# Outlook stage: TensorE's other work cut into pieces behind the replications, the next chunk's softmax chain moved, a fourth accumulating transfer, filler matmuls in idle slots

## The chip, the cores and the metric

The kernel runs on one core of one Trainium2 chip, in one launch. The metric is the device time of the whole launch in microseconds (us). The kernel before takes 4110.46 us (median of three runs, 4110.16 to 4110.85). The engines are named as the profile names them: PE is TensorE (matmuls; PEld its weight loads), DVE is VectorE, ACT is ScalarE, POOL is GpSimd, SP is SyncE.

## The reference, cut to what matters

The input is a batch of 16 images of 56 x 56 pixels and 192 channels. Two blocks follow each other, each on a group-normalised input and with a residual. The first, an "outlook attention", is the one that the change touches:

```python
def _L0_conv_ref(x_map, W_attn, b_attn, W_v, b_v, W_proj, b_proj):   # heads 6, K 3, 32 channels a head
    a = x_map @ W_attn + b_attn
    a = jax.nn.softmax(a.reshape(B, H * W, heads, k * k), axis=-1)      # 9 weights per pixel and head
    v = x_map @ W_v + b_v
    vp = jnp.pad(v, ((0, 0), (pad, pad), (pad, pad), (0, 0)))
    patches = jnp.stack([vp[:, i:i + H, j:j + W, :] for i in range(k) for j in range(k)], axis=3)
    y = jnp.einsum('bpKhd,bphK->bphd', patches, a)                      # sum over the 9 taps
    return y.reshape(B, H, W, C) @ W_proj + b_proj

x = x + _L0_conv_ref(_gn(x), ...)
x = x + _L1_conv_ref(_gn(x), ...)      # shifted 7 x 7 window attention, 12 heads
```

## The kernel before

The 16 images are taken in 8 pairs. A pair fills the partitions: 2 x 192 channels are three tiles of 128, called j = 0, 1, 2, where tile 1 holds 64 channels of each image (`LO` and `HI` are its halves). A loop over the 8 pairs has two stages: the outlook stage (about 173 us of the 502 us of a pair in the trace) and the window attention stage. The change touches the outlook stage alone.

The outlook stage goes through 7 chunks of 8 image rows (448 pixels), c = 0 to 6. In a chunk the nine taps k = 0 to 8 are 14 operations (`OPS`, `NOPS`). For operation n, PE replicates the softmax weights over the channels with one or two bf16 matmuls against a selection matrix (`reps`, line 409), into one of two pairs of PSUM banks, and DVE multiplies this by the shifted values (`product`, line 1237) into a slot of `prod`. `reps(c, n)` waits until product n-2 is done, since it takes the banks of that one. So PE can be two operations ahead of DVE, no more. Below, "slot n" of a chunk is the replication n and what PE does behind it until replication n+1.

The nine products are summed in two ways. POOL issues three DMAs that add one slot of `prod` to another (`merge`, line 1438: tap 1 onto 0, 3 onto 2, 5 onto 4; 672 KB each), and adds the rest itself (`add`, line 1453) into `psum_p` and at last `y0`. `FREED` says after which add a slot of `prod` may be written again; DVE waits for that, and for the transfers (`merged`), before a product.

Beside the replications PE does for the next chunk, c+1: `logits` (matmuls of the normalised input `xn` with W_attn), `values_wide` and `values_middle` (with W_v), `turn_logits` (transposes), and after the softmax `turn_weights` (transposes of the three bf16 parts of the weights, kept by ACT into `at`). And for the chunk before, c-1: `residual`, `project_halves`, `project_outer`, `project_middle` (the residual by an identity matmul, then W_proj). The order in which these stand between the replications is written by hand: by the `if n == ...` in `outlook` of PE, of DVE (softmax pieces) and of ACT. Each engine works strictly down its list, so an instruction that waits holds up all that stand behind it, the replications too. A matmul of 128 rows and 448 columns in fp32 goes as two records in the trace; two matmuls on the two halves of the array (as lines 334 and 335) run beside each other, below "a half pair".

In chunk 0 there is nothing to project, in chunk 6 nothing to prepare. Behind chunk 6 stand `finish_last` on DVE and two short additions on POOL (the last sums), then the last projection. `stay_warm` are matmuls whose result nobody reads.

Of the kernel before, what the change touches and what calls it, by code (L numbers as in the profile page):

```python
# [9 lines left out]
ALU = mybir.AluOpType  # L10
# [3 lines left out]
B, H, W, C = 16, 56, 56, 192  # L14
# [7 lines left out]
T = 3  # L22
LO, HI = slice(0, 64), slice(64, 128)
ORDER = (0, 2, 1)

OHEADS, KK = 6, 9
# [6 lines left out]
CHUNKS = H // ROWS  # L33
CT = ROWS * W
# [4 lines left out]
MERGES = 3  # L39
# [13 lines left out]
SUM_ORDER = (0, 2, 6, 8, 4, 7)  # L53
FREED = {0: 1, 2: 1, 6: 2, 3: 3, 4: 4, 7: 5}
# [26 lines left out]
def mixer(nc, x, wa, ba, wv, bv, wp, bp, wqkv, bqkv, wo, bo, table, sel_in, gmat_in, mask_in, out):  # L81
    ctx = ExitStack()
    with ctx:
# [202 lines left out]
        def _(pe):  # L286
# [43 lines left out]

            def logits(G, bank):
                pe.wait_ge(xn_ok, ONE + T * (G + 1))
                pe.wait_ge(a_kept, ONE + 2 * G)
                mm(P[LO, bank, 0:CT], wa_s[:, 0, :], xn[:, 0, :], start=True, stop=False)
                mm(P[HI, bank, 0:CT], wa_s[:, 2, :], xn[:, 2, :], start=True, stop=False)
                mm(P[LO, bank, 0:CT], wa_s[LO, 1, :], xn[LO, 1, :], start=False, stop=True)
                mm(P[HI, bank, 0:CT], wa_s[HI, 1, :], xn[HI, 1, :], start=False, stop=True).then_inc(l_mm, 1)
# [6 lines left out]
            def values_middle(bank):  # L344
                middle(bank + 1, wv_s, 0, 3, xn, CT).then_inc(v_mm, 1)

# [50 lines left out]
            with pe.Fori(0, NP) as i:  # L397
# [15 lines left out]
                def residual(c, tiles):  # L413
                    for j in tiles:
                        mm(P[:, V_BANK + j, 0:CT], ident[:], xa[:, j, c * ROWS:(c + 1) * ROWS, 0:W],  # L415
                           start=True, stop=False)

                def project_halves(c):
                    if c < CHUNKS - 1:
# [20 lines left out]

                def outlook(c):
                    G = G0 + c
                    more = c < CHUNKS - 1
                    for n in range(NOPS):
                        reps(c, n)
                        if more:
                            if n == 0:
                                logits(G + 1, SOFT_BANK)
                            elif n == 1:
                                pe.wait_ge(a_kept, ONE + 2 * G + 2)  # L450
                                pe.wait_ge(x1_kept, ONE + T * (G - 1 if c else G))
                                values_wide(V_BANK)
                            elif n == 2:
                                turn_logits(G + 1, SOFT_BANK)
                            elif n == 4:
                                values_middle(V_BANK)
                        if c > 0:
                            if n == 5:
                                pe.wait_ge(v_kept, ONE + T * (G + 2 if more else G + 1))
                                pe.wait_ge(x1_kept, ONE + T * (G - 1))  # L460
                                residual(c - 1, (0,))
                            elif n == 6:
                                residual(c - 1, (2, 1))
                            elif n == 7:
                                project_halves(c - 1)
                            elif n == 8:
                                project_outer(0)
                            elif n == 9:
                                project_outer(2)
                            elif n == 10:  # L470
                                project_middle(0)
                            elif n == 11:
                                project_middle(1)
                        if more:
# [1132 lines left out]
```

## Time and profile before

| | before |
|---|---|
| median of 3 runs | 4110.46 us |
| the profiled execution: its time / its span | 4108.7 / 4106.8 us |
| PE, DVE, ACT, POOL busy | 86%, 68%, 46%, 62% of the span |
| granted TensorE clock, mean | 0.918 of full speed |
| transfers `prod` onto `prod` | 168, 672 KB each, median 5.3 us from issue to landing |
| one pair, from the first product of pair 1 to that of pair 2 | 598.16 us on, period about 502 us |
| its outlook stage: first product to last sum | 598.16 to 770.04 us |

The page's shares are averages over two stages with different limits, so they say little of the outlook stage; the trace is read in stretches of one chunk of pair 1. The granted clock has two levels, 1.00 (2.4 GHz) and 0.50 (1.2 GHz); a number between them in a stretch is a mix.

### The profile page before, as it was taken

The numbers are of one execution on the slowest core, as the hardware profiler recorded it, in microseconds if no ns is written. First come the engines' busy times: TensorE is split into PE (matmuls) and PEld (weight loads), VectorE is DVE, ScalarE is ACT, GpSimd is POOL, SyncE is SP. The second block draws the span as 40 slices with busy tenths as digits, with TensorE's granted clock in tenths as the row PEclk, the third lists the DMA queues.
The fourth block names the chain that finished last, engine by engine and source line by source line (L and its number), as shares of the span: only waits on it lengthen the run. The fifth ranks groups of instructions, "written<-read, shape, count | busy, mean of one in ns | idle before, by whom it ended". The sixth has DMA issues, their size and how long they took to land.

```text
span 4106.8 us, 107056 instructions
## 1 busy us (share of the span) xinstructions
PE 3542.4 (86%) x39508; PEld 1954.8 (48%) x39508; DVE 2790.4 (68%) x4865; ACT 1897.6 (46%) x4034; POOL 2527.0 (62%) x1878
## 2 busy tenths in 40 slices
PE   4889978899788997889978899788997899978998
PEld 3336643366434663346633466335662356523565
DVE  2767757677576775857757577585776767667676
ACT  2325643355433554336633455334653255532555
POOL 0757737577375773757737577375764767556674
PEclk8989989899798997989979899798998999988998
DMA  3432214322242222422224222341223422134121
GB/s 73 88 71 67 77 47 88 66 63 75 52 88 60 70 70 62 90 55 75 72 54 88 52 75 70 63 90 46 76 68 68 81 59 77 53 78 85 50 76 56
DMA packets 199422, 284.55 MB, mean 69 GB/s; under 512 B 18136, under 2 KB 177368, under 8 KB 198872
## 3 DMA queue, kind: packets, MB, share of 16 engines
q0 software_dynamic: 24192, 115.62, 14.4%
q1 hardware_dynamic: 168992, 160.51, 13.2%
q8 instruction: 343, 5.62, 0.6%
q10 hardware_dynamic: 5688, 1.11, 0.2%
q14 instruction: 207, 1.70, 0.1%
HBM read 45.97 MB, written 38.54 MB: 21 GB/s over the span
## 4 chain that ended last, share of the span: by engine, by line
PE 58%; issue 14%; DVE 11%; ACT 9%; POOL 5%; DVEq 1%; ACTq 0%; DMA 0%; POOLq 0%
PE P L292 5%; PE P L294 5%; PE P L409 4%; PE P L582 4%; PE P L599 4%; PE P L553 4%; PE P L415 3%; DVE prod L1237 3%; PE P L295 3%; PE P L532 3%; PE P L301 3%; PE P L535 2%; PE P L300 2%; PE P L617 2%; POOL sp__70 L1522 2%
## 5 line engine op out<-in xcount | busy, mean ns | idle before, releaser
L1237 DVE TENSOR_TENSOR prod<-P,vpad 128x896 f32<-128x896 f32 (+1 forms) x784 | 807.2, 1048 | 343.8 <-PE P L409 342.2
L1515 POOL TENSOR_TENSOR sp__70<-sp__70,mx 128x588 f32<-128x588 f32 x512 | 599.9, 1172 | 622.2 <-DVE mx L1309 621.9
L1522 POOL TENSOR_TENSOR sp__70<-sp__70,rc 128x588 f32<-128x588 f32 x512 | 600.3, 1172 | 54.6 <-DVE rc L1319 54.6
L409 PE MATMUL P<-at,sel 108*128 108x448 bf16 x1512 | 453.9, 384 | 131.4 <-DVE prod L1237 71.2
L1438 POOL DMA_DIRECT2D prod<-prod x168 | 148.7, 885 | 660.3 <-DVE prod L1237 649.9
L1299 DVE TENSOR_TENSOR sp__70<-P,relb 128x196 f32<-128x196 f32 x512 | 184.7, 361 | 498.0 <-PE P L553 497.7
L974 ACT ACTIVATE pt<-P 98x294 f32<-98x294 f32 x1024 | 430.2, 421 | 200.6 <-PE P L582 197.8
L1453 POOL TENSOR_TENSOR psum_p<-psum_p,prod 128x1344 f32<-128x1344 f32 x152 | 461.8, 3038 | 11.9
L582 PE MATMUL P<-ident,sp__70 113*98 113x113 f32 x3072 | 399.2, 267 | 49.0 <-POOL sp__70 L1522 36.3
L1316 DVE TENSOR_REDUCE sm<-sp__70 128x12 f32<-128x588 f32 x512 | 387.3, 756 | 44.0 <-ACT sp__70 L964 43.9
L582 PEld LDWEIGHTS P<-ident,sp__70 113*98 113x98 f32 x3072 | 329.9, 131 | 145.4 <-POOL sp__70 L1522 71.8
L1309 DVE TENSOR_REDUCE mx<-sp__70 128x12 f32<-128x588 f32 x512 | 389.5, 761 | 9.4
L964 ACT ACTIVATE sp__70<-sp__70 128x588 f32<-128x588 f32 x512 | 360.6, 704 | 29.2 <-POOL sp__70 L1515 27.9
L409 PEld LDWEIGHTS P<-at,sel 108*128 108x128 bf16 x1512 | 115.5, 100 | 512.9 <-DVE prod L1237 270.9
L553 PE MATMUL P<-kbd,qs 32*64 32x98 f32 x12288 | 305.5, 264 | 24.7 <-ACT kbd L948 12.6
L1302 DVE TENSOR_TENSOR sp__70<-P,relb 128x392 f32<-128x392 f32 x512 | 284.5, 556 | 0.0
L958 ACT ACTIVATE vs<-P 98x192 f32<-98x192 f32 x512 | 126.7, 333 | 294.7 <-PE P L532 294.7
L553 PEld LDWEIGHTS P<-kbd,qs 32*64 32x64 f32 x12288 | 205.0, 133 | 111.2 <-issue 95.2
L1508 POOL TENSOR_SCALAR xr<-xa,bout 128x392 f32<-128x392 f32 x192 | 246.5, 1285 | 0.0
L599 PE MATMUL P<-pt,vbd 98*32 98x49 f32 x12288 | 221.2, 218 | 24.6 <-ACT pt L974 18.0
L415 PE MATMUL P<-xa,ident 128*128 128x448 f32 x336 | 164.0, 604 | 75.4 <-ACT vpad L840 74.8
L898 ACT ACTIVATE xa<-P,bias 128x448 f32<-128x448 f32 x168 | 106.7, 635 | 262.9 <-PE P L428 209.2
(185 smaller groups left out, 7507.8 us busy)
## 6 DMA issues: line engine op xcount, KB each, us to landing
prod<-prod POOLq DMA_DIRECT2D x168, 672.0 KB, 5.3
vbd<-vs SPq DMA_DIRECT2D x512, 147.0 KB
xin<-in_x SPq DMA_DIRECT2D x126, 336.0 KB, 4.0
out<-ot SPq DMA_DIRECT2D x184, 168.0 KB, 2.2
out<-ot SPq DMA_DIRECT2D x80, 84.0 KB
wn<-in_L_conv_qkv_weight SPq DMA_DIRECT2D x2, 432.0 KB, 6.4
wno<-in_L_conv_proj_weight SPq DMA_DIRECT2D x2, 144.0 KB, 6.5
self<-in_sel ACTq DMA_DIRECT2D x3, 91.1 KB
```

Of the source, the lines that this page charges most:

```text
L409: last = mm(P[:, 2 * (n % 2) + b, 0:CT], sel[:, k, :], at[:, col:col + CT], start=True, stop=True)
L553: last = mm(P[half * SLOT:(half + 1) * SLOT, r, part * 2 * N:(part + 1) * 2 * N], qs[rows, w % 2, j, tok:tok + SLOT], kbd[rows, w % 2, j, ...
L582: last = turn(P[0:2 * N, bank, c * QUERIES:(c + 1) * QUERIES], sp_[0:QUERIES, s % SOFTS, g * 2 * N:(g + 1) * 2 * N], ident[0:QUERIES, 0:QU ...
L599: last = mm(P[32 * r:32 * r + 32, Y_BANK, col:col + N], vbd[w % 2][:, 2 * p + half, m, 2 * HD * g:2 * HD * (g + 1)], pt[:, (q + m) % KEPT, ...
L964: go(sp_[:, s % SOFTS, :], sp_[:, s % SOFTS, :], ACT.Exp).then_inc(p_exp, 1)
L974: go(pt[:, (STEPS * w + s) % KEPT, 3 * b:3 * b + 3, :, :], src, ACT.Copy).then_inc(p_kept, 1)
L1237: tt(by_row(dst), by_row(P[:, b:b + len(op), 0:CT]), val, ALU.mult).then_inc(prod_ok, 1)
L1309: red(mx[:, b, :], sp_[:, b, :].rearrange("p (h k) -> p h k", h=NH), AX.X, ALU.max).then_inc(t_max, 1)
L1316: red(sm[:, b, :], sp_[:, b, :].rearrange("p (h k) -> p h k", h=NH), AX.X, ALU.add).then_inc(p_sum, 1)
L1453: tt(y0[:] if n == PADD - 1 else psum_p[:], slot(0) if n == 0 else psum_p[:], slot(k), ALU.add).then_inc(padd_ok, 1)
L1515: tt(per_head(sp_[:, b, :]), per_head(sp_[:, b, :]), spread(mx[:, b, :]), ALU.subtract).then_inc(t_sub, 1)
L1522: tt(per_head(sp_[:, b, :]), per_head(sp_[:, b, :]), spread(rc[:, b, :]), ALU.mult).then_inc(p_norm, 1)
```

## The change

In words:

- PE: `logits` is cut in two (slots 0 and 1 in place of slot 0 alone), the values in five pieces (slots 2, 4, 5, 5, 6 in place of 1 and 4), the order of value tiles becomes 0, 1, 2 (`V_ORDER`). The residual moves from slots 5 and 6 to 7 and 8, the projection from 7 to 11 to slots 9, 10 and 12, tiles in the order 2, 0, 1 (`P_ORDER`). `turn_weights` part 0 moves from slot 12 to 11.
- PE: two filler matmuls (`stay_warm(2, ...)`) in slots 8, 9, 10 and 12 of chunk 0, and in all slots but 7, 8, 9, 10 and 12 of chunk 6.
- DVE: softmax pieces from slots 3, 4, 6, 7, 9, 11 to 4, 5, 6, 7, 8, 9; the three statistics from slots 0, 1, 2 to 0, 5, 10.
- POOL: a fourth transfer a chunk (tap 7 onto 6) in place of one addition, in all chunks but the last; order of the additions changed; the last sums of the stage take tap 6 where they took tap 4.
- ACT: `back` part 1 ahead of the first `keep_x1`, `keep_weights` part 0 ahead of the last.

The core of the diff:

```diff
-MERGES = 3
+MERGES = 4
 PADD = KK - 1 - MERGES
-SUM_ORDER = (0, 2, 6, 8, 4, 7)
-FREED = {0: 1, 2: 1, 6: 2, 3: 3, 4: 4, 7: 5}
+FREED = {0: 1, 2: 1, 3: 2, 4: 3, 6: 4}
...
+                def prepare(c, n):
+                    G = G0 + c
+                    if n < 2:
+                        logits_part(G + 1, n, SOFT_BANK)
+                    elif n == 2:
+                        pe.wait_ge(a_kept, ONE + 2 * G + 2)
+                        pe.wait_ge(x1_kept, ONE + T * (G - 1 if c else G))
+                        values_halves(V_BANK)
+                    elif n == 3:
+                        turn_logits(G + 1, SOFT_BANK)
+                    elif n == 4:
+                        values_square(V_BANK)
+                    elif n == 5:
+                        values_outer(0, V_BANK)
+                        values_rest(V_BANK)
+                    elif n == 6:
+                        values_outer(2, V_BANK)
+                    elif n == 11:
+                        turn_weights(G + 1, 0, SOFT_BANK)
+                    elif n == 13:
...
+                        turn_weights(G + 1, 1, V_BANK)
+
+                def project(c, n):
+                    G = G0 + c
+                    if n == 7:
+                        if c < LAST:
+                            pe.wait_ge(v_kept, ONE + T * (G + 1) + 1)
+                        pe.wait_ge(x1_kept, ONE + T * (G - 1))
+                        residual(c - 1, 0)
+                    elif n == 8:
+                        if c < LAST:
+                            pe.wait_ge(v_kept, ONE + T * (G + 1) + 3)
+                        residual(c - 1, 2)
+                        residual(c - 1, 1)
+                    elif n == 9:
+                        project_halves(c - 1)
+                        project_middle(0)
+                    elif n == 10:
+                        project_outer(2)
+                        project_outer(0)
+                    elif n == 12:
+                        project_middle(1)
+
                 def outlook(c):
                     for n in range(NOPS):
                         reps(c, n)
+                        if c < LAST:
+                            prepare(c, n)
+                        elif n not in (7, 8, 9, 10, 12):
+                            stay_warm(2, SOFT_BANK)
                         if c > 0:
+                            project(c, n)
+                        elif n >= 8 and n not in (11, 13):
+                            pe.wait_ge(v_kept, ONE + T * (G0 + 2))
+                            stay_warm(2, V_BANK)
...
@@ ACT
                         back(G + 1, 0, SOFT_BANK)
+                        back(G + 1, 1, SOFT_BANK)
                     if c > 0:
                         keep_x1(c - 1, 0)
-                    if more:
-                        back(G + 1, 1, SOFT_BANK)
-                    if c > 0:
-                        keep_x1(c - 1, 1)
-                        keep_x1(c - 1, 2)
-                    if more:
-                        keep_weights(G + 1, c + 1, 0, SOFT_BANK)
+                        keep_x1(c - 1, 1)
+                    if c < LAST:
+                        keep_weights(G + 1, c + 1, 0, SOFT_BANK)
+                    if c > 0:
+                        keep_x1(c - 1, 2)
+                    if c < LAST:
                         keep_weights(G + 1, c + 1, 1, V_BANK)
...
@@ DVE
-                        if c >= 2 and n < T:
-                            stat_x1(c - 2, n)
+                        if c >= 2 and n in (0, 5, 10):
+                            stat_x1(c - 2, n // 5)
                         if more:
-                            if n == 3:
+                            if n == 4:
                                 soft_max(G + 1, SOFT_BANK)
-                            elif n == 4:
+                            elif n == 5:
                                 soft_shift(G + 1, SOFT_BANK)
                             elif n == 6:
                                 soft_sum(G + 1, SOFT_BANK)
-                            elif n in (7, 9, 11):
-                                soft_split(G + 1, (n - 7) // 2, SOFT_BANK)
+                            elif n in (7, 8, 9):
+                                soft_split(G + 1, n - 7, SOFT_BANK)
...
@@ POOL
                     if c > 0:
-                        add(c - 1, 2)
-                        add(c - 1, 3)
+                        add(c - 1, 1, 8)
+                        add(c - 1, 2, 4)
                     merge(c, 0)
                     if c > 0:
-                        add(c - 1, 4)
+                        add(c - 1, 3, 6)
                     else:
                         pool.wait_ge(tail_ok, ONE + 5 * i)
                     merge(c, 1)
                     merge(c, 2)
-                    add(c, 0)
-                    add(c, 1)
+                    add(c, 0, 2)
+                    if c < CHUNKS - 1:
+                        merge(c, 3)
```

How the rows stand on PE in chunk 1, from replication 5 on. Line 409 (after: 433) are the replications, 415 (438) the residual, 423 and 424 the projection's first half pair, 361 a value tile, 368 and 369 the last half pair of value tile 1. Before:

```order
L406 REGISTER_ALU
L409 MATMUL P<-at,sel 128x448 x2
L415 MATMUL P<-xa,ident 128x448
L406 REGISTER_ALU
L409 MATMUL P<-at,sel 128x448 x2
L415 MATMUL P<-xa,ident 128x448 x2
L406 REGISTER_ALU
L409 MATMUL P<-at,sel 128x448 x2
L420 ISA
L423 MATMUL P<-y_68,wp_s 128x448
L424 MATMUL P<-y_68,wp_s 128x448
```

After:

```order
L433 MATMUL P<-at,sel 128x448 x2
L361 MATMUL P<-xn,wv_s 128x448
L368 MATMUL P<-xn,wv_s 64x448
L369 MATMUL P<-xn,wv_s 64x448
L430 REGISTER_ALU
L433 MATMUL P<-at,sel 128x448 x2
L361 MATMUL P<-xn,wv_s 128x448
L430 REGISTER_ALU
L433 MATMUL P<-at,sel 128x448 x2
L496 REGISTER_ALU
L438 MATMUL P<-xa,ident 128x448
```

The residual, which waits for ACT to have taken the values out of its banks, stood behind replication 5 and stands behind 7; the work that was done before slot 5 now fills slots 5 and 6.

On POOL, from the wait ahead of a chunk's first addition to the first transfer of the next chunk (chunks 1 to 2; `L1453`, after `L1496`, are additions). Before:

```order
L1452 ISA
L1453 TENSOR_TENSOR psum_p<-prod 128x1344
L1449 REGISTER_ALU
L1452 REGISTER_ALU
L1453 TENSOR_TENSOR psum_p<-psum_p,prod 128x1344
L1449 REGISTER_ALU
L1452 REGISTER_ALU
L1453 TENSOR_TENSOR psum_p<-psum_p,prod 128x1344
L1452 REGISTER_ALU
L1453 TENSOR_TENSOR psum_p<-psum_p,prod 128x1344
L1436 ISA
L1438 DMA prod<-prod 128x1344
```

After:

```order
L1495 ISA
L1496 TENSOR_TENSOR psum_p<-prod 128x1344
L1478 REGISTER_ALU
L1480 DMA prod<-prod 128x1344
L1488 REGISTER_ALU
L1495 REGISTER_ALU
L1496 TENSOR_TENSOR psum_p<-psum_p,prod 128x1344
L1495 REGISTER_ALU
L1496 TENSOR_TENSOR psum_p<-psum_p,prod 128x1344
L1478 ISA
L1480 DMA prod<-prod 128x1344
L1490 ISA
```

One addition has become the issue of a transfer, right behind the first addition.

## Rows read from the trace of the kernel before

**Rows 1.** Windows by chunk: length, PE, PEld, DVE, ACT, POOL busy, granted clock, DMA share, GB/s.

```profile
598.16:622.38 24.22, 18.82 (x67) 5.95 (x69) 17.36 (x21) 7.37 (x12) 6.44 (x5) 0.71 0.44 86
622.38:647.41 25.03, 22.13 (x89) 7.93 (x91) 17.37 (x21) 9.16 (x15) 18.92 (x9) 0.92 0.42 83
694.59:718.17 23.58, 20.15 (x89) 7.69 (x91) 18.97 (x24) 9.16 (x15) 17.78 (x9) 1.00 0.45 89
741.76:761.87 20.11, 17.44 (x51) 6.24 (x50) 15.92 (x17) 3.38 (x5) 16.09 (x9) 0.75 0.53 103
```

**Rows 2.** Groups on DVE, chunk 4: busy, mean ns of one, idle before, releaser.

```profile
L1237 DVE TENSOR_TENSOR prod<-P,vpad 128x896 f32<-128x896 f32 (+1 forms) x14 | 14.4, 1047 | 4.6 <-PE P L409 4.6
```

**Rows 3.** Timeline of PE, chunk 4: start, duration, instruction, idle before it.

```profile
695.38 0.59 PE L336 MATMUL P<-xn,wa_s 64*64 64x448 f32 x1
...
696.28 0.55 PE L409 MATMUL P<-at,sel 108*128 108x448 bf16 x2
696.77 0.64 PE L292 MATMUL P<-xn,wv_s 64*128 64x448 f32 x1
...
697.72 1.02 PE L294 MATMUL P<-xn,wv_s 128*128 128x448 f32 x2
...
699.71 0.60 PE L350 MATMUL P<-ident,lg 128*112 128x128 f32 x4
700.15 0.54 PE L409 MATMUL P<-at,sel 108*128 108x448 bf16 x2
...
705.73 1.02 PE L415 MATMUL P<-xa,ident 128*128 128x448 f32 x2 [1.98 <-ACT vpad L840]
...
710.29 0.92 PE L428 MATMUL P<-y,wp_s 128*128 128x448 f32 x2
711.04 0.54 PE L409 MATMUL P<-at,sel 108*128 108x448 bf16 x2
711.42 0.92 PE L428 MATMUL P<-y,wp_s 128*128 128x448 f32 x2
...
715.80 0.62 PE L359 MATMUL P<-identb,comb 112*108 112x112 bf16 x8 [0.32 <-DVE comb L1156]
716.26 0.35 PE L409 MATMUL P<-at,sel 108*128 108x448 bf16 x1
...
717.59 0.55 PE L409 MATMUL P<-at,sel 108*128 108x448 bf16 x2 [0.77 <-ACT at L859]
```

**Rows 4.** Timeline of POOL, chunks 4 and 5.

```profile
712.29 0.86 POOL L1438 DMA_DIRECT2D prod<-prod  x1 [5.29 <-DVE prod L1237]
712.86 3.37 POOL L1453 TENSOR_TENSOR psum_p<-prod 128x1344 f32<-128x1344 f32 x1
716.31 9.26 POOL L1453 TENSOR_TENSOR psum_p<-psum_p,prod 128x1344 f32<-128x1344 f32 x3
725.50 0.87 POOL L1438 DMA_DIRECT2D prod<-prod  x1
726.11 3.33 POOL L1453 TENSOR_TENSOR y<-psum_p,prod 128x1344 f32<-128x1344 f32 x1
729.71 0.87 POOL L1438 DMA_DIRECT2D prod<-prod  x1 [0.27 <-issue]
```

**Rows 5.** Line 1438 (the transfers), outlook stage of pair 1, 21 of them.

```profile
DMA to landing us min/median/max: 5.2/5.3/7.1
```

**Rows 6.** Timeline of PE, start of chunk 0.

```profile
597.20 0.93 PE L409 MATMUL P<-at,sel 108*128 108x448 bf16 x2 [3.73 <-issue]
598.06 1.01 PE L334 MATMUL P<-xn,wa_s 128*64 128x448 f32 x1
...
599.75 1.01 PE L336 MATMUL P<-xn,wa_s 64*64 64x448 f32 x1
```

**Rows 7.** Timeline of POOL and DVE, end of the stage.

```profile
758.49 3.04 POOL L1453 TENSOR_TENSOR psum_p<-prod 128x1344 f32<-128x1344 f32 x1 [0.78 <-DMA prod<-prod]
...
767.64 2.40 DVE L1270 TENSOR_TENSOR y<-psum_p,prod 128x448 f32<-128x448 f32 x3
```

More of the change, by code:

```diff
@@ L33 @@
 CHUNKS = H // ROWS
+LAST = CHUNKS - 1
 CT = ROWS * W
@@ L329, in turn_x, with logits_part @@
                 last.then_inc(x_turned, 1)
-            def logits(G, bank):
[L332 to L337, printed above, removed]
+            def logits_part(G, part, bank):
+                if part == 0:
+                    pe.wait_ge(xn_ok, ONE + T * (G + 1))
+                    pe.wait_ge(a_kept, ONE + 2 * G)
+                    mm(P[LO, bank, 0:CT], wa_s[:, 0, :], xn[:, 0, :], start=True, stop=False)
+                    mm(P[HI, bank, 0:CT], wa_s[:, 2, :], xn[:, 2, :], start=True, stop=False)
+                else:
+                    mm(P[LO, bank, 0:CT], wa_s[LO, 1, :], xn[LO, 1, :], start=False, stop=True)
+                    mm(P[HI, bank, 0:CT], wa_s[HI, 1, :], xn[HI, 1, :], start=False, stop=True).then_inc(l_mm, 1)
+            def logits(G, bank):
+                logits_part(G, 0, bank)
+                logits_part(G, 1, bank)
             def values_wide(bank):
@@ L411, in reps, with residual @@
                     last.then_inc(rep_mm, 1)
[L413 to L416, printed above, removed]
+                def residual(c, j):
+                    mm(P[:, V_BANK + j, 0:CT], ident[:], xa[:, j, c * ROWS:(c + 1) * ROWS, 0:W],
+                       start=True, stop=False)
                 def project_halves(c):
-                    if c < CHUNKS - 1:
+                    if c < LAST:
                         pe.wait_ge(padd_ok, ONE + PADD * (G0 + c + 1))
@@ L441, in outlook @@
                 def outlook(c):
-                    G = G0 + c
-                    more = c < CHUNKS - 1
                     for n in range(NOPS):
                         reps(c, n)
-                        if more:
[L447 to L454, printed above, removed]
-                            elif n == 4:
-                                values_middle(V_BANK)
-                        if c > 0:
[L458 to L473, printed above, removed]
-                        if more:
-                            if n == 12:
-                                turn_weights(G + 1, 0, SOFT_BANK)
-                            elif n == 13:
-                                if c > 0:
-                                    pe.wait_ge(x1_kept, ONE + T * (G - 1) + 1)
-                                else:
-                                    pe.wait_ge(v_kept, ONE + T * (G + 2))
-                                turn_weights(G + 1, 1, V_BANK)
@@ L489, in _ @@
                 pe.wait_ge(x1_kept, ONE + T * (G0 + c))
-                residual(c, (0, 2, 1))
+                for j in ORDER:
+                    residual(c, j)
                 stay_warm(8, SOFT_BANK)
```

72 lines of the change are left out of this document (43 added, 29 removed).

## The prediction

> **What bounds the kernel now.** The page's shares mix two stages, so I read the outlook stage chunk by chunk. First the windows: chunks 0, 1, 4 and 6 of pair 1 take 24.22, 25.03, 23.58 and 20.11 us [rows 1]; chunks 2, 3 and 5 repeat chunk 4 within 0.02 us. In chunk 4 DVE is busy for 18.97 and PE for 20.15 of 23.58 us at full clock: no engine is full, so something makes them take turns. The groups on DVE say what: the 14 products had 4.6 us of idle time before them, all of it ended by a replication, and no other group on DVE had any [rows 2]. The timeline of PE shows why the replications came late. PE stands at the residual for 1.98 us, until ACT has emptied the value banks, and the replications of the later slots stand behind it; 0.32 us go to a wait for the softmax weights and 0.77 us to one for ACT's copy of them [rows 3]. Before that, PE had given out its work in lumps: half pair, half pair and two full tiles behind replications 0 and 1, where DVE, only two operations behind, runs dry. In chunks 0, 1 and 6 the granted clock is 0.71, 0.92 and 0.75, that is, 14.0, 4.0 and 10.1 us at the lower level (twice the missing share times the length) [rows 1].
>
> So three rings bound a chunk: DVE's work, PE's work, and POOL's list with its transfers. The change smooths the first two; I price each ring.
>
> **Part by part, a steady chunk (2 to 5).** DVE: the operations stay the same in number and kind, only their slots change. 23.58 - 4.6 = 19.0 us.
>
> PE: the matmuls are the same too, cut otherwise. From starts in [rows 3]: a replication pair 0.38 (711.04 to 711.42), a full tile 0.75 (710.29 to 711.04), a half pair 0.90 to 0.95 (695.38 to 696.28; 696.77 to 697.72), 0.11 more where a half pair follows a replication (696.28 to 696.77 is 0.49), `turn_logits` 0.44, `turn_weights` part 0 0.46, part 1 about 0.25. Sum: 27 replications 5.1, 8 full tiles 6.0, 7 half pairs 6.4, five entries 0.5, transposes 1.15: 19.2 us. What waits stay? The residual now stands in slots 7 and 8. Going through the slots with these prices, PE reaches the residual of slot 8 some 10.9 us into the chunk; the last value tile is multiplied by 9.6, ACT does `exp` at about 9.5 (DVE's shift stands in slot 5, behind a statistic) and the last copy by 10.6. The wait goes to nothing, with 0.3 us to spare. `turn_weights` finds its input ready (the last split is two slots earlier). But one wait comes out that was hidden: `logits` part 0 takes the bank from which ACT copies the last third of the weights, transposed in slot 13. About 0.5 us of ACT and the hand-overs stand against one replication pair: 0.4 us. PE's ring is 19.6 us; by subtraction (23.58 less the waits shown, 3.1, and 0.4 at other replications) it is 20.1. I take 19.8.
>
> At one place the Trainium skill speaks against the cutting: "TensorE: Matmul & The Clock Gate", Part 3, The mechanism, says that a weight load overlaps running matmuls only if it goes to other rows of the array. By that, each change from a full tile to a replication would expose a weight load, and a chunk has one such boundary more: about 0.1 us a chunk, 4 us in all. The starts here show no exposed load there: 0.38 us for two streams of 0.19 [rows 3]. I add nothing.
>
> POOL: one addition of 3.1 us (9.26 / 3) becomes the issue of a transfer that holds POOL for 0.57 (712.29 to 712.86) [rows 4]. But a new ring forms. DVE may write slot 0 of the next chunk when the first addition is done; that waits for transfer 1 (tap 3 onto 2); that is issued behind the third addition of the chunk before. Around it: first addition 3.45, issue of transfer 3 0.57, two additions 6.17, issue 0.61, the addition into `y0` up to the issue of transfer 1 3.60 (726.11 to 729.71) [rows 4], landing 5.3 [rows 5], and 0.25, my allowance for the hand-over: 19.95 us. With the shortest landing (5.2) it is 19.85, with the longest (7.1) 21.75. The transfers are no bound: 0.45 of 23.58 us for three is 3.5 us each [rows 1], so four fill 14 of 20 us.
>
> The longest ring sets the chunk: 20.0 us, PE and POOL together. Gain 3.6 us in each of four chunks: 14.3.
>
> **Chunk 0.** PE starts at the lower level: replication pair 0.86, half pair 1.69 [rows 6]. With `logits` cut, replication 1 starts at 597.20 + 2.55 = 599.75 and replication 2 at 602.30; before, all of `logits` and of `values_wide` stood ahead of it. DVE is then short of work for 1.4, 1.4 and 0.4 us ahead of products 1, 2 and 3, and full after that: 17.4 + 3.2 = 20.6 us against 24.22: gain 3.6.
>
> **Chunk 1.** It has no statistics, so PE's ring (19.8) bounds it; the additions of chunk 0 are early. Against 25.03 that gains 5.3 us, if the clock is up. The fillers are for that: the clock fell in the second half of chunk 0, where PE had a replication pair each 1.0 to 1.5 us and nothing else. Now the values go on until slot 6, and fillers (two of 512 columns, 0.43 by the price of 448) stand in slots 8, 9, 10, 12. They are hidden: 0.38 + 0.43 is less than a slot of DVE (1.0 to 1.5).
>
> **Chunk 6 and the last sums.** DVE could finish the chunk in 17 to 18.5 us in place of 20.11. But the end is POOL's: the first addition of chunk 6 started 16.7 us after its first product (758.49) [rows 7], and in the new ring it starts at 16.5; one more addition and the two short sums follow as before. The last sum on DVE, which ended at 770.04, 28.3 us after the first product [rows 7], waits for the second of them: 27.3. Gain 1.0, not 2.
>
> **Slow landings.** Of the 21 transfers of pair 1 the longest took 7.1 us [rows 5]; where it is transfer 1 the ring waits. I take off 0.7 us a pair.
>
> Sum a pair: 14.3 + 3.6 + 5.3 + 1.0 - 0.7 = 23.5; eight pairs, 188 us. From the profiled execution's own 4108.7 us this leaves 3920.7; the median of the runs stands 1.8 above it: 3922 us. The attention stage has the same instructions; its phases against the clock's steps shift, with either sign, and I price that at 0 with 10 us to both sides.
>
> Bounds: if POOL's ring counts for less and DVE's bound held (19.0), another 1.0 x 4 x 8 = 32 us would go: 3890. If each landing of transfer 1 took 7.1 us, five chunks a pair would be 1.8 us longer: 72 us, 3994.
>
> **Rivals.**
> 1. The clock falls all the same. For it: in slots 11 and 13 of chunk 0 only short transposes stand, and before slot 8 no filler; it fell at the head of chunk 6, which before held nothing but replications. Against it: chunk 4 kept 1.00 through 1.98 us of standstill. Price: chunk 1 would again lose about 2.4 us and chunk 6 about 0.9, where at the lower level a slot with filler (0.86 + 0.86) is longer than DVE's. 3.3 x 8 = 26 us: 3948.
> 2. The fourth transfer stretches POOL's ring: transfers 3, 0 and 1 now follow each other in 11 us, and a landing near 7 us becomes the rule. For it: landings of 7.1 exist [rows 5]. Against: each fills the engines for 3.5 us and the nearest two are issued 4.2 apart, as before (725.50, 729.71) [rows 4]. Up to 72 us: 3994, and DVE idle before the first product of each chunk, ended by POOL.
> 3. Slower than before, by one mechanism: the residual of slot 8 waits for the last value copy, which stands on ACT behind `exp`, which waits for DVE's shift, now one slot later and behind a statistic. All replications from 9 on stand behind that wait on PE, and DVE behind them. I find 0.3 us to spare. If the copy is d late, chunks 1 to 5 grow by d - 0.3. A pair gains 19.6 us in chunks 1 to 5 less 5 (d - 0.3), and 4.6 in chunk 0 and the end: from d = 5.1 it is slower than before, and at d = 6 by 4.5 us a pair: 4146. Against it: the wait is 1.98 us today with the residual two slots earlier.
>
> **Chances.** Forecast 0.60; rival 1 0.24; rival 2 0.11; rival 3 0.05. Range: the forecast's own 3900 to 3940; with rival 1 whole, rival 2 for the most part and the DVE bound: 3893 to 3985. A measurement of this kernel tells 0.2% (8 us) from no change. Faster 0.94, same 0.02 (a mix of rivals 2 and 3), slower 0.04.
>
> **What would show it.** Right: steady chunks of 19.7 to 20.3 us, no wait for the value copy before the residual, a short wait of `logits` for the copy of the weights, idle of DVE under 1.5 us a chunk, the granted clock 1.00 from the middle of chunk 0 to the last sums; chunk 0 near 20.6, chunk 1 near 19.8. Wrong: chunks over 21 us; DVE idle ended by POOL or a transfer at product 0 (rival 2); PE idle at the residual of slot 8 (rival 3); a clock share under 0.95 in chunk 1 or 6 (rival 1).

## The result and the profile after

| | before | after |
|---|---|---|
| median of 4 runs, us | 4110.31 (4109.11 to 4110.85) | 3893.97 (3893.10 to 3895.59) |
| profiled execution, us: time, span | 4108.7, 4106.8 | 3895.59, 3893.4 |

The ratio is 0.9475, interval [0.9458, 0.9491]: 5% faster, 216 us. The forecast was 3922 with a range of 3893 to 3985: the time lies in it, but only 1 us above its lower bound, and outside the 3900 to 3940 that the prediction gave for its own sum. 28 us more were gained than forecast, 3.5 a pair.

By the starts of the chunks' first products in the two traces, summed over the eight pairs (the 100 us ahead of the very first product, 100.4 before and 100.2 after, are left out):

| stretch | before, us | after, us | change | forecast |
|---|---|---|---|---|
| chunk 0 | 190.7 | 162.8 | -27.9 | -28.8 |
| chunk 1 | 199.9 | 155.3 | -44.6 | -42.4 |
| chunks 2 to 5, slow landings with them | 754.8 | 630.2 | -124.6 | -108.8 |
| chunk 6 and last sums | 226.1 | 218.7 | -7.4 | -8 |
| attention stage and the rest | 2635.0 | 2626.3 | -8.7 | 0 |

The windows after, pair 1, chunks 0, 1, 3, 6 and the last sums, in the columns of [rows 1]:

```profile
572.70:593.51 20.81, 17.92 (x75) 6.14 (x77) 17.43 (x22) 7.46 (x12) 6.67 (x5) 0.88 0.51 100
593.51:612.93 19.42, 19.37 (x87) 7.82 (x87) 17.54 (x22) 9.24 (x15) 15.39 (x8) 1.00 0.73 143
632.61:652.22 19.61, 19.49 (x87) 7.87 (x87) 18.84 (x25) 9.29 (x15) 15.53 (x8) 1.00 0.72 142
691.44:709.16 17.72, 16.76 (x66) 6.07 (x65) 15.46 (x17) 2.18 (x4) 13.89 (x8) 1.00 0.75 146
709.16:718.90 9.74, 5.86 (x19) 2.39 (x19) 9.55 (x6) 1.22 (x2) 9.39 (x6) 0.93 0.09 19
```

A steady chunk took 23.58 us and takes 19.61, and PE, busy for 20.15 of 23.58 us before, is busy for 19.49 of 19.61: it hardly stands still. The granted clock, 0.92 in chunk 1 and 0.75 in chunk 6 before [rows 1], is 1.00 in both; in chunk 0 it rose from 0.71 to 0.88. The group of products on DVE in chunk 3, which answers to [rows 2]:

```profile
L1280 DVE TENSOR_TENSOR prod<-P,vpad 128x896 f32<-128x896 f32 (+1 forms) x14 | 14.4, 1043 | 0.7 <-PE P L433 0.6
```

Same work, and 0.7 us of idle time before it where 4.6 stood. On PE, in chunk 3 (line 433 is a replication, 438 the residual, 383 `turn_weights`, 337 `logits`), the residual, and then the last transposes of the weights and the head of the next chunk:

```profile
642.72 0.54 PE L433 MATMUL P<-at,sel 108*128 108x448 bf16 x2
643.10 1.67 PE L438 MATMUL P<-xa,ident 128*128 128x448 f32 x4
644.60 0.54 PE L433 MATMUL P<-at,sel 108*128 108x448 bf16 x2
...
651.19 0.37 PE L383 MATMUL P<-identb,comb 112*108 112x112 bf16 x4
651.62 0.55 PE L433 MATMUL P<-at,sel 108*128 108x448 bf16 x2
652.23 0.59 PE L337 MATMUL P<-xn,wa_s 128*64 128x448 f32 x1
```

No wait stands at the residual, where 1.98 us stood [rows 3]; the replication pair still takes 0.38 (642.72 to 643.10). From the last replication pair to `logits` it is 0.61 (651.62 to 652.23), where an entry into a half pair took 0.49 (696.28 to 696.77 in [rows 3]): the new wait for the weights' copy is 0.12 us, not the 0.4 of the forecast. On POOL, chunks 3 and 4, against [rows 4] (a DMA row is the issue of a transfer):

```profile
639.37 3.35 POOL L1496 TENSOR_TENSOR y<-psum_p,prod 128x1344 f32<-128x1344 f32 x1
642.37 1.19 POOL L1480 DMA_DIRECT2D prod<-prod  x1
646.61 0.86 POOL L1480 DMA_DIRECT2D prod<-prod  x1 [3.05 <-DVE prod L1280]
648.20 3.04 POOL L1496 TENSOR_TENSOR psum_p<-prod 128x1344 f32<-128x1344 f32 x1 [0.73 <-DMA prod<-prod]
651.18 0.87 POOL L1480 DMA_DIRECT2D prod<-prod  x1
652.27 6.15 POOL L1496 TENSOR_TENSOR psum_p<-psum_p,prod 128x1344 f32<-128x1344 f32 x2 [0.22 <-DVE prod L1280]
```

The addition into `y0` starts at 639.37 and the issue of transfer 1 at 642.37: 3.00 us, where 3.60 stood in the sum. The landings of the stage's 27 transfers, against [rows 5], and those of the last two of them, transfers 1 and 2 of chunk 6:

```profile
DMA to landing us min/median/max: 5.3/5.4/8.4
DMA to landing us min/median/max: 5.6/7.0/8.4
```

The 8.4 us are transfer 2 of chunk 6, issued 0.6 us behind transfer 1. Transfer 1, the one that the forecast's ring waits for, landed after 5.6 us in chunks 2 and 3 of all pairs and after 5.7 to 6.5 in chunks 4 and 5.

### The profile page after: what moved, and what is told of

The parts are those of the page before. It is cut to its first block, busy times and chain, and to the rows that moved or that the text cites. A ratio compares the mean times of both kernels' runs of the same rounds, so it can differ in the third digit from the quotient of the medians.

```text
span 3893.4 us, 107608 instructions
## 1 busy us (share of the span) xinstructions
PE 3493.4 (90%) x39716; PEld 1962.9 (50%) x39716; DVE 2794.1 (72%) x4865; ACT 1905.6 (49%) x4034; POOL 2423.8 (62%) x1878
## 3 DMA queue, kind: packets, MB, share of 16 engines
q0 software_dynamic: 31104, 148.65, 19.5%
## 4 chain that ended last, share of the span: by engine, by line
PE 59%; issue 11%; DVE 11%; ACT 8%; POOL 6%; DMA 2%; ACTq 0%; DVEq 0%; POOLq 0%
PE P L433 5%; PE P L625 5%; PE P L642 4%; PE P L294 4%; PE P L296 4%; PE P L596 4%; DVE prod L1280 3%; PE P L575 3%; PE P L303 3%; PE P L578 2%; PE P L302 2%; PE P L660 2%; POOL sp__70 L1566 2%; ACT kbd L988 2%; PE P L297 2%
## 5 line engine op out<-in xcount | busy, mean ns | idle before, releaser
L1480 POOL DMA_DIRECT2D prod<-prod x216 | 202.7, 958 | 499.1 <-DVE prod L1280 495.7
L433 PE MATMUL P<-at,sel 108*128 108x448 bf16 x1512 | 426.4, 361 | 58.7 <-DVE prod L1280 30.5
L1005 ACT ACTIVATE sp__70<-sp__70 128x588 f32<-128x588 f32 x512 | 360.8, 705 | 29.2 <-POOL sp__70 L1559 27.9
L1496 POOL TENSOR_TENSOR psum_p<-psum_p,prod 128x1344 f32<-128x1344 f32 x104 | 328.1, 3154 | 9.2 <-DVE prod L1280 3.0
L596 PE MATMUL P<-kbd,qs 32*64 32x98 f32 x12288 | 304.8, 264 | 25.3 <-ACT kbd L989 12.7
L1496 POOL TENSOR_TENSOR psum_p<-prod 128x1344 f32<-128x1344 f32 x56 | 172.4, 3079 | 83.8 <-DMA prod<-prod 83.7
```

The lines of the kernel that those rows point to most:

```text
L433: last = mm(P[:, 2 * (n % 2) + b, 0:CT], sel[:, k, :], at[:, col:col + CT], start=True, stop=True)
L596: last = mm(P[half * SLOT:(half + 1) * SLOT, r, part * 2 * N:(part + 1) * 2 * N], qs[rows, w % 2, j, tok:tok + SLOT], kbd[rows, w % 2, j, ...
L1005: go(sp_[:, s % SOFTS, :], sp_[:, s % SOFTS, :], ACT.Exp).then_inc(p_exp, 1)
L1496: tt(y0[:] if n == PADD - 1 else psum_p[:], slot(0) if n == 0 else psum_p[:], slot(k), ALU.add).then_inc(padd_ok, 1)
```

## The experiments

"Ratio" is the time against that of the kernel before, measured beside it. Unless it says otherwise, the edit is made to the changed kernel.

**No fillers** (e1): what they are worth.

```diff
-                        elif n not in (7, 8, 9, 10, 12):
-                            stay_warm(2, SOFT_BANK)
...
-                        elif n >= 8 and n not in (11, 13):
-                            pe.wait_ge(v_kept, ONE + T * (G0 + 2))
-                            stay_warm(2, V_BANK)
```

> The changed kernel without any of the new filler matmuls in chunks 0 and 6; nothing else differs. Theory A (the fillers keep the clock up): the granted clock falls again to the lower level near the end of chunk 0 and at the head of chunk 6; chunk 1 (now 19.4 us) grows by 2 to 3.4 us, chunk 6 and the last sums by about 1: some 26 us in all, 3894 + 26 = 3920. Rival B (the value tiles up to slot 6 and the denser chunks already keep it up): clock 1.00 in chunk 1 and most of chunk 6, time 3894 within 4 us.

Measured 3913.31 us, ratio 0.9519 [0.9503, 0.9535]: 19 us above the changed kernel, where theory A had 26. Windows of chunks 0, 1 and 6:

```profile
574.21:595.32 21.11, 17.86 (x67) 6.09 (x69) 17.52 (x21) 7.45 (x12) 6.99 (x6) 0.74 0.52 101
595.32:616.58 21.26, 21.22 (x87) 8.05 (x87) 17.54 (x21) 9.22 (x15) 15.32 (x8) 0.91 0.65 127
...
696.87:715.50 18.63, 16.56 (x50) 5.89 (x50) 15.50 (x17) 3.40 (x5) 14.44 (x8) 0.82 0.73 142
```

The clock is down again at the head of chunk 1 and PE, busy for 21.22 of 21.26 us, sets its length: 1.8 us a pair. That is 14 of the 19 us; chunk 0 gives another 3.5 over the eight pairs. Chunk 6 is 0.9 longer here, but the last sums are about 1 us shorter, so the stage's end takes as long as with fillers (218.1 against 218.7 us over eight pairs). The fillers do what they are for in chunks 0 and 1; those of chunk 6 bring nothing.

**Three transfers** (e2): POOL's list as before.

```diff
-MERGES = 4
+MERGES = 3
-FREED = {0: 1, 2: 1, 3: 2, 4: 3, 6: 4}
+SUM_ORDER = (0, 2, 6, 8, 4, 7)
+FREED = {0: 1, 2: 1, 6: 2, 3: 3, 4: 4, 7: 5}
...
-                        add(c - 1, 1, 8)
-                        add(c - 1, 2, 4)
+                        add(c - 1, 2)
+                        add(c - 1, 3)
...
-                    add(c, 0, 2)
-                    if c < CHUNKS - 1:
-                        merge(c, 3)
+                    add(c, 0)
+                    add(c, 1)
```

> The changed kernel with POOL's list as it was before (three transfers and five additions a chunk); PE, ACT and DVE as changed, fillers in. Theory A (the fourth transfer is needed because POOL's ring would bound the chunk): the ring is transfer 1 landing 5.6 to 5.8, four additions 3.1 each, transfer issue 0.6, last addition 3.0: 21.8 us a chunk against 19.6; about 2.1 us in each of five chunks of eight pairs: 3894 + 85 = 3979, DVE idle ahead of product 0 and ended by POOL. Rival B (POOL has slack at either number of transfers, PE's list bounds): 3894 within 5 us.

Measured 4009.42 us, ratio 0.975 [0.9734, 0.9767]; chunks 2 and 3 of 21.8 us, as theory A had it, chunks 4 and 5 of 22.2 to 22.5. DVE and POOL at the head of a chunk:

```profile
652.69 1.09 DVE L1279 TENSOR_TENSOR prod<-P,vpad 128x896 f32<-128x896 f32 x1 [1.39 <-POOL psum_p L1495]
```

```profile
643.68 1.17 POOL L1480 DMA_DIRECT2D prod<-prod  x1
...
649.53 3.04 POOL L1495 TENSOR_TENSOR psum_p<-prod 128x1344 f32<-128x1344 f32 x1 [2.86 <-DMA prod<-prod]
...
652.64 9.28 POOL L1495 TENSOR_TENSOR psum_p<-psum_p,prod 128x1344 f32<-128x1344 f32 x3
```

DVE waits for the first addition, which waits for transfer 1, which is issued behind three additions in a row (9.28 us) and the addition into `y0`. The fourth transfer is worth 115 us of the 216: it takes an addition out of the ring. That is 30 us more than expected: chunk 6 with the last sums, not in theory A's sum, is 20 us longer over the eight pairs.

**Only the fourth transfer** (e3), on the kernel before.

```diff
@@ kernel before
-MERGES = 3
+MERGES = 4
...
+                    if c < CHUNKS - 1:
+                        merge(c, 3)
```

> The kernel before with POOL's part of the change alone: the fourth transfer in place of an addition, the order of the additions, the last sums. PE, ACT and DVE as before, no fillers. Theory A (before, each chunk was held by PE's waits and lumps, 23.6 us, over POOL's 22.0): chunks of 23.58 as before, 4110 within 8 us. Rival B (POOL's list was part of the bound): chunks shorter by 1 us or more, 4070 or less.

Measured 4110.44 us, ratio 1.000 [0.999, 1.0009]. The steady chunks stay at 23.58 us, but for two of 25.1 in which the clock falls: with PE's old list the ring of POOL is not the longest, and a shorter one brings nothing. Neither part pays its full value alone: 0 us here, and 101 for the rest without it (e2).

**Only the fillers** (e4), on the kernel before (slots 8 to 11 of chunk 0; 0 to 4, 12 and 13 of chunk 6).

```diff
@@ kernel before
+                        elif 8 <= n <= 11:
+                            pe.wait_ge(v_kept, ONE + T * (G0 + 2))
+                            stay_warm(2, V_BANK)
+                        if not more and (n < 5 or n >= 12):
+                            stay_warm(2, SOFT_BANK)
```

> The kernel before with fillers alone: two filler matmuls behind replications 8 to 11 of chunk 0 and 0 to 4, 12 and 13 of chunk 6; order, softmax pieces and POOL as before. Theory A (the fillers are worth what the lower clock costs in chunk 1 and chunk 6): clock at 1.00 in chunk 1, which goes from 25.0 to about 23.2 us, chunk 6 from 20.1 to 19.1; with the end bound by POOL about 2 to 2.5 us a pair, 4110 - 18 = 4092. Rival B (too thin between slots 5 and 8 of chunk 0 to hold the clock, or the fillers run at the lower clock and delay replications): 4110 within 8 us or slower.

Measured 4109.46 us, ratio 0.9996 [0.9987, 1.0006]: nothing. Windows of chunk 1, of chunk 2, and of 3.4 us inside chunk 2:

```profile
622.38:645.44 23.06, 20.16 (x89) 7.70 (x91) 17.37 (x21) 9.16 (x15) 18.79 (x9) 1.00 0.46 90
645.44:670.72 25.28, 21.85 (x89) 8.26 (x91) 19.18 (x25) 9.20 (x15) 17.84 (x9) 0.93 0.42 82
657.80:661.20 3.40, 3.40 (x6) 1.34 (x6) 2.06 (x3) 0.68 (x2) 0.05 (x1) 0.50 0.90 180
```

```profile
656.58 1.02 PE L415 MATMUL P<-xa,ident 128*128 128x448 f32 x2 [1.98 <-ACT vpad L845]
...
657.85 3.19 PE L415 MATMUL P<-xa,ident 128*128 128x448 f32 x4
```

Chunk 1 gains the 2 us, and chunk 2 loses 1.7: the clock fell to its lower level (share 0.50) just after PE's 1.98 us at the residual, and the residual's next two matmuls (four rows of the trace) took 3.19 us, not 1.67. In seven of the eight pairs chunk 3 or chunk 4 takes 25.1 to 25.3 us as well. Over the eight pairs chunks 2 to 5 lose 25 us, and the rest of the kernel gains as much. The same standstill cost no clock in chunk 4 of the kernel before, at 1.00 [rows 1]. No theory foresaw that. The spread list has no such standstill, which may be a second use of it; no run isolates that.

**The wait of `logits` loosened** (e5), **transfer 1 ahead of the third addition** (e6), **both** (e7).

```diff
@@ e5, e7 (logits_part gets parts=2 as an argument)
-                    pe.wait_ge(a_kept, ONE + 2 * G)
+                    pe.wait_ge(a_kept, ONE + 2 * G + parts - 2)
...
-                        logits_part(G + 1, n, SOFT_BANK)
+                        logits_part(G + 1, n, SOFT_BANK, 1 if c else 2)
@@ e6, e7
-                    if c > 0:
-                        add(c - 1, 3, 6)
-                    else:
+                    if c == 0:
                         pool.wait_ge(tail_ok, ONE + 5 * i)
                     merge(c, 1)
+                    if c > 0:
+                        add(c - 1, 3, 6)
```

> The changed kernel, where the first half of logits (slot 0, chunks 1 to 5) waits only for ACT's copy of the first part of the softmax weights, the one that shares its bank, and no more for the second. Measured: PE stands there for 0.23 us, and has no other wait in a chunk of 19.61. Theory A (two rings almost level: PE 19.61, POOL with transfer 1 about 19.45): chunks of 19.45, 0.16 x 5 x 8 = 6 us less: 3888. Rival B (PE alone bounds): 0.23 less: 19.38, 3885. Rival C (POOL's ring is the bound and the wait is its shadow): 3894 within 2 us.

> The changed kernel, where POOL issues transfer 1 ahead of the addition into y0 and no more behind it; nothing else differs. It is issued 1.3 us earlier but queues behind transfer 0, so it lands about 0.4 earlier; y0 comes 2 us later, with 2.4 to spare. Theory A (PE's ring, 19.61, bounds; POOL's 19.45 does not): steady chunks 19.61; only the chunks that grew to 19.8 to 20.1 by slow landings (7 of 32 in chunks 4 and 5) shrink, and the last sums by up to 0.4 us a pair: 3894 - 2 - 3 = 3889. Rival B (POOL's ring bounds): 0.38 less in each of five chunks: 3879.

> Both edits together: logits waits for the first part alone, and transfer 1 is issued ahead of the addition into y0. Theory A (two rings almost level): with both shortened the chunk falls to PE's bare list, 19.38; 0.23 x 5 x 8 = 9, and 4 for slow landings and the last sums: 3881, more than the first edit alone. Rival B (PE alone): the same as the first edit alone plus 4. Rival C: no change, 3894.

Measured: e5 3892.76 us, 0.9472 [0.9459, 0.9485], not to be told from the changed kernel; e6 3890.64, 0.9467 [0.9454, 0.9480]; e7 3885.07, 0.9453 [0.944, 0.9466]. In e5 chunks 2 and 3 are 19.49, that is 0.12 us less and not the 0.23 that the expectation took for the wait, and chunks 4 and 5 of all pairs but one still grow, up to 20.3; in e6 chunks 4 and 5 hardly grow any more (19.64); in e7 nearly all are at 19.49, not at the 19.38 expected. In e6 and e7 the last sums are 1.3 us shorter and chunk 6 is 0.4 longer. A steady chunk of e7:

```profile
629.48:648.97 19.49, 19.45 (x89) 7.87 (x91) 18.84 (x25) 9.29 (x15) 15.61 (x8) 1.00 0.73 143
```

So there are two bounds close to each other: PE's list with its 0.12 us wait, and POOL's ring, which takes over where transfer 1 lands late. In the steady chunks each edit alone meets the other bound. By the profiled executions, of what e7 gains some 6 us are its shorter end of the stage, which e6 has as well (212.8 against 218.7 us over eight pairs), and some 6 are in chunks 2 to 5 (624.4 against 630.2).

**No residual in chunks 0 to 5** (e8; left out: the residual matmuls, and with them that term of the output; the projection then starts the sum in its banks). It asks how far PE's list is the bound.

```diff
-                        residual(c - 1, 0)
...
-                        residual(c - 1, 2)
-                        residual(c - 1, 1)
```

> The changed kernel without the residual matmuls of chunks 0 to 5 (the first block's residual is left out there): 2.25 us of PE less in each of chunks 1 to 6; all else the same. Theory A (POOL's ring stands right behind PE's): chunks fall only from 19.61 to about 19.45: 3894 - 7 = 3887, with DVE idle ended by POOL or PE idle at y0. Rival B (DVE's 19.0 is the next bound): 0.6 x 5 x 8 = 24 less: 3870. Rival C (PE alone bounds and nothing stands behind it): 2.25 x 5 x 8 = 90 less: 3804.

Measured 3918.91 us, ratio 0.9533 [0.9519, 0.9548]: 25 us slower than the changed kernel, with less work. Two stretches of the outlook, not aligned to chunks, and two rows of PE in the second:

```profile
597.00:616.00 19.00, 17.55 (x83) 6.65 (x81) 17.58 (x22) 9.01 (x15) 14.57 (x8) 1.00 0.74 145
616.00:637.00 21.00, 18.98 (x81) 6.89 (x81) 18.86 (x25) 9.10 (x16) 16.39 (x10) 0.92 0.67 132
```

```profile
626.30 0.55 PE L433 MATMUL P<-at,sel 108*128 108x448 bf16 x2 [0.51 <-DVE prod L1278]
628.25 0.55 PE L433 MATMUL P<-at,sel 108*128 108x448 bf16 x2 [1.39 <-DVE prod L1278]
```

Chunks at full clock take 19.0 to 19.7, but in chunks 2, 3 and 5 the clock falls for a while and they take 21.0 to 21.2. PE is busy for 90% of such a chunk, but just before the fall, where the residual stood, it stands 0.51 and 1.39 us for DVE; the half pair behind the second wait already runs at the lower level. Neither theory foresaw that, and the run doesn't settle the bound.

**The residual replaced by four filler matmuls** (e9; left out: as in e8), **and with the edits of e7** (e10).

```diff
-                        residual(c - 1, 0)
+                        stay_warm(1, V_BANK)
...
-                        residual(c - 1, 2)
-                        residual(c - 1, 1)
+                        stay_warm(3, V_BANK + 2)
```

> The changed kernel with the residual of chunks 0 to 5 left out, as in the run without it, but four bf16 filler matmuls (0.86 us) in its place in slots 7 and 8: PE's list is 1.4 us shorter, 18.1 us a chunk, and not idle there. Theory A (the run without the residual was slower because the clock fell in chunks 2, 3 and 5 for one step each; at full clock POOL's ring bounds): clock 1.00 in all steady chunks, each 19.45 to 19.7, 3894 within 7 us. Rival B (leaving the residual out costs by another way, through the buffers): chunks of 21 us again, 3919. Rival C (only PE bounded): 18.2 to 19.0 a chunk, 3870 or less.

> The same, and with the two edits of the faster version (logits waits for the first part of the weights alone; transfer 1 ahead of the addition into y0). PE's list 18.1, POOL's ring about 19.07, DVE's work 18.97 us a chunk. Theory A (three rings, each the next bound): chunks of 19.0 to 19.2, 3885 - 0.4 x 5 x 8 = 3869. Rival B (POOL's list does not matter): as the run before. Rival C: the clock falls, 3900 or more.

Measured: e9 3896.72 us, 0.9479 [0.9465, 0.9494], the changed kernel's time with a list of PE that is 1.4 us shorter. Its chunk 3, DVE's first product of it, and POOL from one first addition to the next:

```profile
633.64:653.07 19.43, 18.29 (x85) 6.88 (x83) 18.84 (x24) 9.28 (x15) 15.55 (x9) 1.00 0.73 143
```

```profile
633.65 1.09 DVE L1280 TENSOR_TENSOR prod<-P,vpad 128x896 f32<-128x896 f32 x1 [0.27 <-POOL psum_p L1496]
```

```profile
630.48 3.04 POOL L1496 TENSOR_TENSOR psum_p<-prod 128x1344 f32<-128x1344 f32 x1 [1.73 <-DMA prod<-prod]
633.47 0.86 POOL L1480 DMA_DIRECT2D prod<-prod  x1
634.07 6.44 POOL L1496 TENSOR_TENSOR psum_p<-psum_p,prod 128x1344 f32<-128x1344 f32 x2
640.46 0.85 POOL L1480 DMA_DIRECT2D prod<-prod  x1
641.07 3.31 POOL L1496 TENSOR_TENSOR y<-psum_p,prod 128x1344 f32<-128x1344 f32 x1
644.05 1.16 POOL L1480 DMA_DIRECT2D prod<-prod  x1
...
649.87 3.04 POOL L1496 TENSOR_TENSOR psum_p<-prod 128x1344 f32<-128x1344 f32 x1 [1.54 <-DMA prod<-prod]
```

DVE's first product now waits for POOL, and POOL waits for nothing in its ring but the landing of transfer 1: the ring takes 19.39 us (630.48 to 649.87), right behind PE's list. That holds for chunks 2 and 3, which are 19.4 in most pairs. In chunks 4 and 5, where transfer 1 lands after 6.0 to 6.5 us and not 5.6, they are 19.7 to 20.3. e10 measured 3888.02, 0.946 [0.9446, 0.9475]: PE's list short and POOL's ring opened, and the chunks are 19.49 again, as in e7. 3869 was expected, and that missed. DVE, then PE, of e10:

```profile
632.27 1.09 DVE L1280 TENSOR_TENSOR prod<-P,vpad 128x896 f32<-128x896 f32 x1 [0.15 <-PE P L433]
633.71 2.09 DVE L1280 TENSOR_TENSOR prod<-P,vpad 128x896 f32<-128x896 f32 x2 [0.35 <-PE P L433]
```

```profile
639.40 0.55 PE L433 MATMUL P<-at,sel 108*128 108x448 bf16 x2 [0.29 <-DVE prod L1280]
...
641.35 0.55 PE L433 MATMUL P<-at,sel 108*128 108x448 bf16 x2 [0.75 <-DVE prod L1280]
```

Now PE waits for DVE in the middle of the chunk, and DVE has 0.15 + 0.35 us of idle time in slots 1 and 2, where PE's pieces (1.4 us a slot) are longer than DVE's product (1.0). DVE is busy for 18.84 of the 19.50 us from 629.40 to 648.90; most of the rest is this idle time. A third ring ends at the same length as the first two.

**The old slots of the softmax and the statistics on DVE** (e11).

```diff
-                        if c >= 2 and n in (0, 5, 10):
-                            stat_x1(c - 2, n // 5)
+                        if c >= 2 and n < T:
+                            stat_x1(c - 2, n)
...
-                            if n == 4:
+                            if n == 3:
...
-                            elif n in (7, 8, 9):
-                                soft_split(G + 1, n - 7, SOFT_BANK)
+                            elif n in (7, 9, 11):
+                                soft_split(G + 1, (n - 7) // 2, SOFT_BANK)
```

> The changed kernel with DVE's softmax pieces and statistics in their old slots (3, 4, 6, 7, 9, 11 and 0, 1, 2); PE, ACT and POOL as changed. Theory A (the splits had to move, since turn_weights moved to slot 11 on PE): PE stands in slot 11 for the last split, about 1.9 us a chunk, with replications 12 and 13 behind it; chunks of 21.5 us, 3894 + 1.9 x 5 x 8 = 3970. Rival B (DVE's slots are a matter of taste, PE's list alone made the gain): 3894 within 5 us.

Measured 4002.30 us, ratio 0.9739 [0.9724, 0.9754]; chunks of 21.5, as expected, some 23.0 with a fall of the clock. PE in slot 11:

```profile
648.08 0.62 PE L383 MATMUL P<-identb,comb 112*108 112x112 bf16 x8 [1.70 <-DVE comb L1197]
```

`turn_weights`, one slot earlier than before, waits 1.70 us for the last split, and the replications stand behind it. Moving DVE's chain is worth 108 us: PE's new list needs it. The 32 us beyond the 3970 expected are for the most part the clock's: chunk 0 takes 22.5 us in the mean, not 20.3, with some 9 us at the lower level in it, not 4 to 5.

**Matmuls around the last transposes of a pair** (e12, on e7), to bring the clock up before chunk 0.

```diff
+                pe.wait_ge(v_kept, ONE + T * (Gn + 1))
+                stay_warm(8, 0)
                 turn_weights(Gn, 0, FIRST_BANK)
+                stay_warm(2, 0)
                 pe.wait_ge(a_kept, ONE + 2 * Gn + 1)
                 turn_weights(Gn, 1, FIRST_BANK)
+                stay_warm(6, 0)
```

> The faster version (3885) with fillers in PE's idle time at the end of a pair: eight ahead of the last transposes of the weights, two between their parts, six behind. Chunk 0 starts at the lower clock and takes 20.6 us, where at full clock (pair 0) it takes 17.5. Theory A (the lower clock at the start comes from the 4.3 and 1.1 us of standstill before): chunk 0 at 18 to 18.7 us in most pairs, 3885 - 15 = 3870. Rival B (the 3.3 us of standstill at the loop's end, which no filler reaches, make the clock fall again inside chunk 0): chunk 0 within 0.5 us of 20.6 or longer, 3885 within 5 us.

Measured 3881.79 us, ratio 0.9443 [0.9430, 0.9455]. Chunk 0 of pair 1:

```profile
569.32:590.17 20.85, 17.96 (x75) 6.16 (x77) 17.43 (x22) 7.45 (x12) 6.68 (x5) 0.88 0.51 100
```

The clock in chunk 0 is 0.88, as in the changed kernel: it did not work there. The 3 us against e7 sit in the attention stage (2620 against 2625 us), and the intervals of the two overlap. For chunk 0 that is rival B. e12 is the fastest version measured; what beats the changed kernel with a reason shown is e7, by 9 us (its runs, 3882.51 to 3886.33, lie all below the changed kernel's 3893.10 to 3895.59).

## Why the prediction was right, and where it was off

- **The lumps and the standstill were the stall**: right. The steady chunks fell by 3.97 us where 3.6 were forecast. DVE's idle time went from 4.6 to 0.7 us a chunk (forecast: under 1.5), the waits at the residual and for the softmax weights are gone, and e11 shows the price of one of them kept (1.70 us in slot 11, 108 us in all).
- **POOL's ring, "the addition into `y0` up to the issue of transfer 1 3.60 (726.11 to 729.71)"**: the step that failed. 3.60 was no duration but held a wait: the issue needs product 5, which in the kernel before ended on DVE at 729.13, 0.58 ahead of the issue's row.

```profile
728.05 1.08 DVE L1237 TENSOR_TENSOR prod<-P,vpad 128x896 f32<-128x896 f32 x1
```

  After, it is 3.00 (639.37 to 642.37). That makes the ring about 19.4 and not 19.95, and e9 shows it: 19.39. Other terms were off too, and cancel. By e9's rows the first addition up to the issue behind it holds 2.99 us, not 3.45, the two additions 6.39, not 6.17, and the landing with its hand-over 5.82 (644.05 to 649.87), not 5.55. Where transfer 1 lands late, in chunks 4 and 5, e9's ring is 19.7 to 20.3, the length forecast for all.
- **PE's list, "I take 19.8"**: the sum from the starts came to 19.6, and 19.61 was measured, but that is luck. Bare the list is 19.49 and not 19.2 (part 1 of `turn_weights` alone holds 0.43, 651.19 to 651.62, not 0.25), and the wait of `logits` is 0.12 and not 0.4. PE's list, and not "PE and POOL together" at 20.0, sets the steady chunk of the changed kernel: 0.39 us less in most of 32 chunks, some 12 us of the 28. Changes from a full tile to a replication, counted in the rows, are five a chunk before and after, not one more as the prediction has it, and none shows a cost: 0.76 us from a full tile to the replication behind it (641.96 to 642.72 in chunk 3), where a full tile was priced at 0.75.
- **Slow landings, 0.7 us a pair**: chunks 2 to 5 together are 2.7 us longer than 32 times 19.61 (630.2 against 627.5), where 5.6 were taken; that is 3 us. Rival 2's mechanism exists (transfer 1 lands after up to 6.5 us, and chunks 4 and 5 take up to 20.1), at a small part of its price of up to 72 us, which took 7.1 us for each landing.
- **Chunk 1, "PE's ring (19.8) bounds it"**: 19.42, so 2 us more over the eight pairs. **Chunk 0** (20.6; measured 20.35 in the mean, 20.81 in pair 1) was right within 0.3 us, and by its mechanism: DVE waits 1.46, 1.42 and 0.34 us ahead of products 1, 2 and 3 (575.25, 577.77 and 579.20 in pair 1), where 1.4, 1.4 and 0.4 were forecast. **The end** (27.3 us from the first product of chunk 6; 27.46, 718.90 - 691.44) was right in its size, but the 27.3 don't follow from the start of the first addition at 16.5 that was given for them: with the 11.55 us that followed it before (758.49 to 770.04) they would be 28.05. That hit is luck as far as the record shows.
- **The attention stage, 0 with 10 us to both sides**: 8.7 us shorter, with the same instructions. Its time at the lower level of the clock fell from 396 to 377 us over the eight pairs, which goes the same way; in e12, whose fillers stand at its end, it is 353 us, and the stage with the rest takes 2620 us. That the stage's phases shifted with its start is the likely cause; no run isolates it. Without these 8.7 us the time would be about 3903, so it is they that bring it to the range's edge.
- **The fillers** (e1: 19 us; rival 1's price for their failing was 26) and **rival 3** (no wait at the residual of slot 8): as argued. Rival 1's 0.9 us for chunk 6 cost nothing at the stage's end. Of the signs named, the steady chunks (19.61, not 19.7 to 20.3) and the last sums in pair 1 (clock 0.93, not 1.00) fell just outside.

By size: of the 28 us, 16 lie in chunks 2 to 5 with their landings, 9 in attention and 2 in chunk 1; chunk 0 and the end take 1 to 2 back, and the last 3 are the two profiled executions' distances from their medians. What stays open is why transfer 1 lands later in chunks 4 and 5 than in 2 and 3, and what ACT's new order is worth: no run puts it, or PE's new order alone, back.

## What to carry to other kernels

Price a ring from durations and known hand-overs, never from the distance of two starts, unless nothing is waited for between them: that distance can hold a wait of the old schedule that the change removes. When three rings of a loop lie within 1% of each other (19.4, 19.5 and 19.6 us here, with a landing of 5.6), a single edit meets the next one at once, and parts don't add up (0 us for the fourth transfer alone, 101 for all the rest without it, 216 for both): look for the next ring before pricing the first. And an interleave is right when no slot on the feeding engine is longer than the same slot on the fed one: the last 0.5 us of idle time on DVE are the two slots where it is.

## What the runs showed of the hardware

- Taking three full tiles (3 x 0.75 = 2.25 us) of matmuls a chunk from PE made the kernel 25 us slower (e8), since the granted clock then fell inside chunks in which PE was busy for 90%, just after it had stood for 0.51 and 1.39 us; four small matmuls in their place brought it back (e9).
- The same standstill of PE, 1.98 us, cost no clock in one place and 1.5 us in another (e4: 3.19 us for two residual matmuls; 1.67 at full clock): a schedule with standstills at full clock may be near losing it.
- The issue of a transfer on POOL overlaps the addition ahead of it: its row starts 3.00 us after an addition that lasts 3.35. And in the one case read it starts 0.58 us after the end of the product it waited for (729.13 to 729.71), which the trace can label as a wait for nothing (the last row of [rows 4]).
- Transfers of 672 KB, all alike, landed after 5.3 to 8.4 us, the longest where one was issued 0.6 us behind another.
